# Attention weights loaded and counted in two parts, 56 warming products with two bridges of 18, and the row numbers of the last expert rounds fetched in one group

## What is computed

```python
h = take(weight, x)                                      # gather of 2048 rows, 1 KB each
h = h + L0_attn(layernorm(h))                            # causal linear attention, 16 heads (q, k, v, then Wout)
h = h + L0_ffn(layernorm(h))                             # one 256 x 256 product, scaled
h = h + L1_attn(layernorm(h))                            # random-feature attention, then relu(x W1) W2
logits = x @ router_w.T; top_idx = argmax(logits)        # L1_ffn: 8 experts, one of them for each token
eo = (silu(xs @ gate[e]) * (xs @ up[e])) @ down[e]       # xs = x * sigmoid(top logit)
h = h + eo + (silu(x @ shared_gate) * (x @ shared_up)) @ shared_down
```

## Time and profile before

| | |
|---|---|
| time, median of 3 runs | 637.1 us (636.89 to 638.11) |
| time of the profiled execution | 642.89 us |
| span in its trace | 641.1 us |
| PE busy | 608.8 us, 95% of the span |
| DVE busy | 496.1 us, 77% |
| ACT busy | 337.5 us, 53% |
| POOL busy | 273.6 us, 43% |
| mean granted TensorE clock | 0.988 of full speed |

### The profile page before, as it was taken

How to read it: one execution, slowest core, us unless ns; L and a number is a source line. 1 busy time by engine, 2 the same in 40 slices (tenths; PEclk the granted TensorE clock), 3 DMA queues, 4 the chain that set the end, 5 groups by cost and what they waited for, 6 DMA issues and landing times.

```text
span 641.1 us, 16205 instructions
## 1 busy us (share of the span) xinstructions
PE 608.8 (95%) x6140; PEld 495.1 (77%) x6140; DVE 496.1 (77%) x1157; ACT 337.5 (53%) x769; POOL 273.6 (43%) x528
## 2 busy tenths in 40 slices
PE   6888899999999999999999999999999979999997
PEld 5666678888889898888989898899899946544543
DVE  2797999899998988888888898876765672475663
ACT  2446575666675655655656545656534112444561
POOL 6262365373474533434252534433422135445433
PEclk8898899999999999999999999999999999999999
DMA  7970000000000000000000000000004455112111
GB/s 250 404 321 1 9 11 9 2 11 10 11 18 1 19 9 11 17 3 18 2 17 3 17 1 19 17 3 17 19 18 124 76 193 183 49 45 67 55 44 37
DMA packets 16013, 34.33 MB, mean 54 GB/s; under 512 B 6449, under 2 KB 11072, under 8 KB 14656
## 3 DMA queue, kind: packets, MB, share of 16 engines
q1 hardware_dynamic: 12064, 24.88, 11.5%
q0 software_dynamic: 3872, 8.41, 4.2%
HBM read 27.43 MB, written 6.63 MB: 53 GB/s over the span
## 4 chain that ended last, share of the span: by engine, by line
PE 81%; DVE 6%; issue 4%; DMA 4%; ACT 3%; POOL 1%; SPq 1%; POOLq 0%; DVEq 0%; ACTq 0%
PE ps L1198 74%; PE ps L1203 3%; PE ps L1359 2%; DMA sorted_ids<-tokens,slot_u 1%; DMA yB<-x_rows,ids 1%; DVE stats L767 1%; DMA H_S<-table,idx_sb 1%; PE ps L1543 1%; ACT qkA L738 1%; DVE rdenTA L842 1%; PE ps L1505 1%; DVE H_S L819 1%; ACT xA L577 0%; DVE qkA L805 0%; PE ps L1333 0%
## 5 line engine op out<-in xcount | busy, mean ns | idle before, releaser
L424 POOL TENSOR_TENSOR var_eps<-mv,ln_eps 128x1 f32<-128x1 f32 x112 | 24.2, 216 | 254.6 <-DVE mv L768 254.2
L1198 PE MATMUL ps<-yTC,we 128*128 128x128 f32 x1024 | 124.3, 275 | 0.0
L1198 PEld LDWEIGHTS ps<-yTC,we 128*128 128x128 f32 x1024 | 120.5, 192 | 1.0 <-issue 0.3
L1198 PE MATMUL ps<-we,yTA 128*128 128x256 f32 (+1 forms) x264 | 84.9, 453 | 0.2 <-ACT yTA L598 0.2
L425 POOL TENSOR_TENSOR rstd<-var_eps,pow_half 128x1 f32<-128x1 f32 x112 | 66.0, 589 | 8.8
L1198 PEld LDWEIGHTS ps<-we,yTA 128*128 128x128 f32 x264 | 49.6, 196 | 20.0 <-issue 15.4
L1198 PE MATMUL ps<-we,ffT 128*128 128x256 f32 x256 | 60.8, 380 | 0.0
L1198 PEld LDWEIGHTS ps<-we,ffT 128*128 128x128 f32 x256 | 47.2, 190 | 5.6
L1198 PE MATMUL ps<-we,yTB 128*128 128x256 f32 (+1 forms) x152 | 43.7, 431 | 0.7 <-issue 0.6
L819 DVE TENSOR_TENSOR H_S<-ps,causal_sb 128x512 f32<-128x512 f32 x64 | 40.0, 667 | 2.4 <-PE ps L1198 2.4
L1198 PEld LDWEIGHTS ps<-yTA,we 128*128 128x128 f32 x256 | 31.7, 202 | 6.1 <-issue 6.1
(11 more groups left out here) (238 smaller groups left out, 1433.3 us busy)
## 6 DMA issues: line engine op xcount, KB each, us to landing
we<-w_experts SPq DMA_DIRECT2D x7, 1536.0 KB, 19.3
we<-w_ff SPq DMA_DIRECT2D x2, 1024.0 KB, 8.7
x_rows<-send_x SPq DMA_DIRECT2D x16, 128.0 KB
home_rows<-send_home SPq DMA_DIRECT2D x16, 128.0 KB
rows_sb<-rows SPq DMA_DIRECT2D x1, 1664.0 KB
we<-w_experts SPq DMA_DIRECT2D x2, 768.0 KB
we<-w_qk SPq DMA_DIRECT2D x2, 512.0 KB
we<-w_v SPq DMA_DIRECT2D x2, 256.0 KB
```

Source lines behind the costliest of these rows:

```text
L424: link(pool.tensor_tensor(var_eps[:, k:k + 1], mv[:, k, 1:2], ln_eps[:], ALU.add))
L1198: return pe.matmul(o, a, b, start=start, stop=stop)
```

## The change

Four things are edited. The q and k weights of the first attention get a semaphore of their own (`qk0_loaded`), on which `a_qk(0)` waits; the weights of v are issued behind the wait for `gathered[0]` and counted by `v0_loaded`, on which `a_v(0)` waits. `WARMING` goes from 48 to 56. Two runs of 18 products of ones by ones are put in on PE, one ahead of `a_s(0)`, one ahead of the wait for `kmax_ready` in `b_kmT(0)`; the second stands behind the wait for `src2T_ready`, which now comes ahead of the wait for `kmax_ready`. And the last two groups of row numbers are one group: `IDS_FROM` loses the border at tile 14, so `load_ids(4)` fetches tiles 10 to 17, and `load_ids(5)` is gone.

```diff
--- before.py
+++ after.py
@@ -58,8 +58,9 @@
     GATE, UP, DOWN = 0, KD * F, 2 * KD * F
     RESIDENT = 4
     ATTENTION = 9 * KD * D - EXPERT
-    WARMING = 48
-    IDS_FROM = [0, MOE_SLOTS, 2 * MOE_SLOTS, 3 * MOE_SLOTS, 5 * MOE_SLOTS, 7 * MOE_SLOTS, TILES]
+    WARMING = 56
+    BRIDGING = 18
+    IDS_FROM = [0, MOE_SLOTS, 2 * MOE_SLOTS, 3 * MOE_SLOTS, 5 * MOE_SLOTS, TILES]
     GROUPS = len(IDS_FROM) - 1
 
     with ExitStack() as ctx:
@@ -203,7 +204,7 @@
         sorted_ids = nc.dram_tensor("sorted_ids", [(E * SPAN + 1) * P, 1], U32, kind="Internal").ap()
 
         names = """idx_loaded small_loaded zero_ready consts_ready
-        qkv0_loaded out0_loaded middle_loaded last_loaded weights_scaled
+        qk0_loaded v0_loaded out0_loaded middle_loaded last_loaded weights_scaled
         residents_loaded experts_ready
         var0_ready var1_ready var2_ready var3_ready var4_ready var5_ready var6_ready
         centre0_ready rstd1_ready centre2_ready centre3_ready rstd4_ready rstd5_ready centre6_ready
@@ -218,7 +219,7 @@
         preC_ready hC_ahead src5T_psum src5T_ready ffa_psum ffb_psum ffa_ready ffb_ready ff2_psum ff2_read
         src6_ready src6T_psum src6T_ready logit_psum logit_copied logit_read tanh_top onehot_ready count_psum counts_read
         slot_ready gate_psum up_psum tanh_gate gC_ready hT_ready sent_ready down_psum tile_done x_kept home_kept ids_scattered
-        ids_cleared ids_loaded0 ids_loaded1 ids_loaded2 ids_loaded3 ids_loaded4 ids_loaded5 table_ready
+        ids_cleared ids_loaded0 ids_loaded1 ids_loaded2 ids_loaded3 ids_loaded4 table_ready
         xT_psum xT_ready eg_psum eu_psum tanh_eg eh_ready ehT_psum ehT_ready ey_psum ey_ready eg_ready
         dve_step pool_step unused""".split()
 
@@ -286,9 +287,9 @@
             sp.dma_start(idx_sb[:], idx).then_inc(S["idx_loaded"], 16)
             for dst, src in ((id_sb[:], ident), (cols_sb[:], cols)):
                 sp.dma_start(dst, src).then_inc(S["small_loaded"], 16)
-            for dst, src in ((qk0_sb, w_qk0), (v0_sb, w_v0)):
-                sp.dma_start(dst, src).then_inc(S["qkv0_loaded"], 16)
+            sp.dma_start(qk0_sb, w_qk0).then_inc(S["qk0_loaded"], 16)
             sp.wait_ge(gathered[0], 16)
+            sp.dma_start(v0_sb, w_v0).then_inc(S["v0_loaded"], 16)
             sp.dma_start(rows_sb, rows.partition_broadcast(P)).then_inc(S["out0_loaded"], 16)
             sp.dma_start(causal_sb[:], causal).then_inc(S["out0_loaded"], 16)
             sp.dma_start(out0_sb, w_out0).then_inc(S["out0_loaded"], 16)
@@ -385,7 +386,6 @@
             load_ids(4)
             late_is_ready(RESIDENT + 2)
             late_is_ready(RESIDENT + 3)
-            load_ids(5)
 
             for s in range(MOE_SLOTS):
                 sp.wait_ge(home_stored[s], 16 * ROUNDS)
@@ -1225,13 +1225,15 @@
 
             def a_qk(t):
                 if t == 0:
-                    pe.wait_ge(S["qkv0_loaded"], 16 * 2)
+                    pe.wait_ge(S["qk0_loaded"], 16)
                 pe.wait_ge(S["src0T_ready"], t + 1)
                 after(pe, "ctx_even", t - 4)
                 after(pe, "ctx_odd", t - 4)
                 by_channel(qk0, yTA, qk0_sb, range(4)).then_inc(S["qk0_psum"], 1)
 
             def a_v(t):
+                if t == 0:
+                    pe.wait_ge(S["v0_loaded"], 16)
                 pe.wait_ge(S["src0T_ready"], t + 1)
                 after(pe, "ffb_ready", (t - 6) * 4 + 4)
                 after(pe, "v0_ready", t)
@@ -1240,6 +1242,8 @@
             def a_s(t):
 
                 if t == 0:
+                    for _ in range(BRIDGING):
+                        matmul(sc[0][:, 0:P], ones_sb[:], ones_sb[:], True, True)
                     pe.wait_ge(S["out0_loaded"], 16 * 3)
                 pe.wait_ge(S["qz_ready"], t * 2 + 2)
                 after(pe, "src5T_ready", t - 4)
@@ -1327,9 +1331,12 @@
 
             def b_kmT(t):
 
-                pe.wait_ge(S["kmax_ready"], t + 1)
                 if t + 1 < T:
                     after(pe, "src2T_ready", t + 2)
+                if t == 0:
+                    for _ in range(BRIDGING):
+                        matmul(km[:, 0:P], ones_sb[:], ones_sb[:], True, True)
+                pe.wait_ge(S["kmax_ready"], t + 1)
                 pe.transpose(km[0:HEADS, 0:P], kmax[:, 0, :], id_sb[:]).then_inc(S["kmaxT_psum"], 1)
 
             def b_kmB(t):
```

## The result

The changed kernel took 650.0 us in the median of four executions (649.33 to 652.3) against 637.61 us (636.89 to 639.28) for before: ratio 1.0197, 95% interval 1.0164 to 1.023, slower by 12.4 us in the medians. It lies inside the range on record (642.0 to 650.5), near its upper end. Timed again later beside 24 executions of before, the ratio was 1.0172 (1.0142 to 1.0202), 649.78 us against 639.55.

The account below looks back on a forecast made before the run. PE's work bounds the middle, step-by-step chains the first 100 and last 130 us. Terms 12.3 + 1.5 - 0.6 - 1.4 - 1.6 - 1.4 + 0.1 = +8.9 us on the median 637.1 gave 646.0 us, range 642 to 650.5.

Parts of the forecast that it names:

- where PE waits for SP's order: Tail, second tile of round 2: PE already waits half a microsecond for SP's increments of `experts_ready`, not for the weights.
- Hold: Tail: the increments come behind all twenty fetches, so PE's second tile of round 2 starts later, +12.3 us.
- Nothing covers this: Tail: no other work hides the 12.3 us, as PE is in order; POOL's need of the merged group costs nothing.
- Restart: Tail, behind the hold: PE comes back at half clock after idling some 13 us, +1.5 us, between 0.8 and 2.6.
- v behind the rows: Start of the fill: v's weights no longer share the DMA engines with the first gather, -0.6 us, from -0.7 to 0.
- The lower number of 0.3: First gather: the gain if each DMA engine takes turns between its queues, 0.3 us instead of 0.6.
- Warming: Fill: eight more warming products shorten the idle time ahead of `a_qk(0)`, which then runs at full clock, -1.4 us.
- First bridge: Fill, ahead of `a_s(0)`: the gap falls to 1.4 us, and `a_s(0)` and `a_qk(1)` run at full clock, -1.6 us.
- Second bridge: Ahead of the `kmax_ready` wait: eight instructions behind it at full clock, -1.4 us, +0.1 for delay; 0.9 at half clock.
- The sum of the fill: v's weights, warming and both bridges together, without hold and restart: -4.9 us.
- the weak step: Carrying the sum from the profiled execution to the median: timed runs may have fewer half-clock stretches to win back.
- The likeliest case: Full hold and most of the clock gains: 646.0 us, own range 643.5 to 649, chance 0.70.

Follow-up runs that it names:

- x1: The change with the two increments of `experts_ready` back behind ten of the twenty fetches, against before: 638.49 us, ratio 0.9961.
- x2: Before with only the two groups of fetches merged, against before: 654.57 us, ratio 1.0231.
- x3: The change with the two increments behind fifteen of the twenty fetches, against before: 645.76 us, ratio 1.0064.
- x5: The change itself, timed again beside 24 executions of before: 649.78 us, ratio 1.0172.
- x9: The change with 190 products of ones on PE ahead of the wait on the increments, against before: 647.27 us, ratio 1.0125.
- x10: x1 timed once more, against before: 635.37 us, ratio 0.9944.
- x6: x1 without bridges and with 48 warming products, so v's weights behind the first rows alone, against before: 637.51 us, ratio 0.9972.
- x7: Before with 56 warming products and nothing else, against before: 638.94 us, ratio 0.9996.
- x4: Before with the two bridges of 18 products alone, against before: 638.55 us, ratio 0.9971.
- x8: The change with expert 7's increment ahead of the twenty fetches and expert 8's behind the fifth, against before: 635.2 us, ratio 0.9932.
- x12: Before, unchanged, profiled once more for a second trace: span 637.4 us.

## Why the prediction was right, and where it was off

**What bounds the kernel, and where PE waits for SP's order: right.** That PE's wait instruction and SP's increments stood within 0.1 us of each other was enough to find the mechanism, though the profile had named nobody. x1, x2 and x3 show it: moved back, alone, and in halves.

**Hold, +12.3 us.** Mis-sized, by the trace: there the wait is 11.38 us, 10.7 more than the 0.64 of before. My bound from the first ten fetches at their own pace, 11.6, was the better one: the twenty took 21.9 us where they had taken 23.1. "Nothing covers this" held, and GpSimd's wait cost nothing.

**Restart, +1.5 us.** 2.05 in the change, 2.0 in x5, 2.2 in x3, 1.6 in x2, 2 to 3 by x9. It was mis-sized by half a microsecond or more. The rule of the Trainium skill's page "TensorE: Matmul & The Clock Gate" that I named, that idle time throttles what follows, agrees with the traces, here with 10.2 us at 0.50. Hold and restart together were 13.8 in the sum. By the trace they are 12.8 against the 0.64 us of before, and 13.4 against x1, where the tile has no wait. In the timed executions the step from x1 and x10 to x5 is 14.0 us (0.022 of 640), and x2 gave 14.8 (0.0231 of 641); each is known to between 2 and 2.5 us, so they agree with the trace and with the sum.

**v behind the rows, -0.6 us.** The statistics start at 7.26 in the mean of the six traces with v ahead and at 6.71 in the eight with v behind: 0.55 us. The lower number of 0.3, which I had worked out from turns between the queues as the page "DMA: Bandwidth & Descriptors" of the Trainium skill has them, is not borne out by the landing; the turns themselves no row shows. What I missed is that `a_qk(0)` may run at full clock with this edit alone, as in x6: I booked that under the warming products alone.

**Warming, -1.4 us.** The effect came, the size did not: `a_qk(0)` ran at half clock in four of the five traces that have neither 56 products nor v behind, and in none of the nine others. x6 and x7 have one edit each and are among the nine, so the second need not add anything; x7 by itself is 0.9996. And where it ran at half clock this delayed `a_s(0)` by 0.9 us and not by 1.4. That the shorter idle time is what keeps the clock is not shown. It was 1.17 to 1.73 us ahead of the first tile in the four traces with the half clock, but 1.31 in x9, 1.57 in x3 and 1.79 in x4, which have none there.

**First bridge, -1.6 us.** Half right. `a_s(0)` or `a_qk(1)` ran at half clock in four of six traces without it and in three of eight with it. The price holds where the clock is kept: from `a_s(0)` to the products behind `a_qk(1)` it is 4.56 us in before and 2.96 in x5. The gap of 1.4 us that I expected behind the bridge was wrong. It is 2.18 us, since a faster `a_qk(0)` only lets PE wait longer for `qz`: without a bridge the gap is 3.18 us in x6 and x7, beside 2.43 in before.

**Second bridge, -1.4 + 0.1.** In 50 to 60 us five of six without it had half clock, one of eight with it. In seven of the eight the transpose follows the maximum within 0.1 us; in x8 the bridge ran at half clock, took 2.10 us and delayed it by 0.9, as I had priced that case. Of the gain of 1.4 us 0.4 came, by the rows from the transpose to those of qf, since PE then waits 0.73 us ahead of 56.71.

**The sum of the fill, -4.9: this is the term that was mis-sized.** The timed executions give 2.5 and 3.6. One part of the error is in the prices. I took what a row lasts longer at half clock for what the kernel loses by it, and for two of the three stretches other waits cover part of that. With the landing's 0.6, 0.9 for `a_qk(0)`, 1.6 for `a_s(0)` and `a_qk(1)` and 0.4 at the second bridge the sum is 3.5. Just so much lies between before and x5 at the first transposes of qf, 61.06 and 57.61. The other part is that not every execution has every stretch, which I had named as the weak step, and that the edits don't remove each of them: the change's own trace has one at 17.9 us. But the profiled execution was no rare one in this. Its mean clock was 0.988, and those of the 72 later ones have medians of 0.988 to 0.990. What takes a part of the 4.2 us between the first part and the end, the runs don't settle: a half-clock stretch at the start of the second part is found in traces of both kinds (x12, x2 and x7; the change, x5, x1, x10 and x3).

**+8.9 forecast, +12.4 and +10.2 measured** in the medians; by its ratio the second is +11.0. The first comparison had four executions of before of 636.9 to 639.3 us, while 72 later ones had medians of 639.4 to 641.1 and ran from 636.0 to 645.9. So some of the 12.4 is where those four fell. What is left over 8.9 is for the most part the fill's term, which was 1.3 to 2.4 us too large. That the sum comes within 1.3 to 3.5 us owes something to luck: by the trace the hold was 1.6 us shorter than my term, which takes up part of what the fill and the restart fell short by.

Two slips of the prediction change nothing in its sum. PE's tenths are at nine from the sixth slice on, not the seventh. And the likeliest case's own range, with its restart of 0.8 to 2.6 and gains of 3.5 to 5.9, is 644.3 to 648.5, not 643.5 to 649.

## What to carry to other kernels

A wait or an increment written behind a row of issues comes no earlier than the row ends, however long its data have been there: before two groups of small transfers are merged, see what stood between them, and who waits for that. Here ten fetches at 1.1 us each stood in front of a signal whose data had long landed. And a gap on TensorE can cost twice, once as time and once as half clock behind it: 11.4 and 2.05 us here. A gain in the clock should be priced by how much earlier the next engine's work or the next step starts, not by how much shorter the row gets, and from several executions.

## What the runs showed of the hardware

The time of one and the same kernel goes with the mean clock that it was granted, though not by that alone. Of 29 executions of before, the two with a mean clock of 0.997 and 0.996 took 637.9 and 637.2 us, the five at 0.981 or 0.983 between 642.6 and 645.9 us; the three at 0.992 lie between 638.6 and 642.5. The places of the half-clock stretches changed from execution to execution with the program unchanged (in the table, before and x12, and the change and x5), which agrees with the page "TensorE: Matmul & The Clock Gate" of the Trainium skill, section "What's actually happening", where the moment of the change of clock varies and the same kernel has another number of slow products from run to run. I had not expected the time of one kernel to spread over 8.7 us in this way, more than six times what I took for the limit of the measurement. Nor had I expected that 190 products of ones, with no use but to be there, shorten a kernel by 2 to 3 us in the middle of a wait.
